# Fourier attention of a decoder layer: plain fp32 phases for the queries, and copies of key and query tiles placed ahead of the folds

## The reference, cut to what matters

```python
q = (x @ Wq.T + bq).reshape(B, L, 16, 32)        # 16 heads of 32; k and v likewise
def fourier(t):                                   # t: [B, L, 16, 32]
    p = einsum('blhd,dm->blhm', t, proj_mat) / sqrt(32)     # 128 phases for each head
    return concatenate([cos(p), sin(p)], -1) / sqrt(128)
kv  = einsum('blhm,blhd->bhmd', fourier(k), v)
out = einsum('blhm,bhmd->blhd', fourier(q), kv)
x   = layernorm(x + out.reshape(B, L, 512) @ Wo.T + bo)
```

## Time and profile before

| | |
|---|---|
| median of 3 runs | 1628.83 us (1627.93 to 1632.57) |
| profiled execution, its own time | 1629.87 us |
| its span in the trace | 1627.5 us |
| TensorE busy | 1564.6 us, 96% of the span |
| TensorE weight loads | 1116.4 us, 69% |
| VectorE busy | 1208.0 us, 74% |
| ScalarE busy | 1113.9 us, 68% |
| GpSimd busy | 715.5 us, 44% |
| mean granted TensorE clock | 0.991 |

### The profile page before, as it was taken

One profiled execution on the slowest core, in us unless ns is written; L12 is line 12 of the kernel. 1 busy time (PEld: TensorE's weight loads), 2 busy tenths in 40 slices (PEclk: granted clock), 3 DMA queues, 4 the chain that ended last, 5 costly groups with the idle time before them and its releaser, 6 DMA issues. The chain is left out here.

```text
span 1627.5 us, 29746 instructions
## 1 busy us (share of the span) xinstructions
PE 1564.6 (96%) x11188; PEld 1116.4 (69%) x11188; DVE 1208.0 (74%) x1849; ACT 1113.9 (68%) x1450; POOL 715.5 (44%) x633
## 2 busy tenths in 40 slices
PE   8999999999999999999999999999799999999996
PEld 6756765676676667667667766765478888888884
DVE  5687577668767766876776687898687777877876
ACT  5796677678667767867777786668256655565664
POOL 4233115203412410340232044373288978898886
PEclk9999999999999999999999999999899999999998
DMA  5100102201210220120022022001512222222211
GB/s 173 53 27 28 52 1 79 79 1 36 83 39 1 79 79 2 52 81 25 1 79 79 2 66 89 30 27 52 150 49 85 85 78 84 84 79 83 78 40 65
DMA packets 49175, 95.75 MB, mean 59 GB/s; under 512 B 3552, under 2 KB 3872, under 8 KB 49056
## 3 DMA queue, kind: packets, MB, share of 16 engines
q1 hardware_dynamic: 39776, 76.67, 15.0%
q10 hardware_dynamic: 9280, 17.31, 2.9%
HBM read 60.38 MB, written 33.59 MB: 58 GB/s over the span
## 5 line engine op out<-in xcount | busy, mean ns | idle before, releaser
L793 DVE SCALAR_TENSOR_TENSOR feat<-feat,phases 128x1024 f32<-128x1024 f32 x256 | 300.9, 1217 | 167.2 <-ACT feat L683 167.1
L683 ACT ACTIVATE feat<-phases 128x1024 f32<-128x1024 f32 x256 | 248.4, 1024 | 127.3 <-PE phases L533 108.2
L690 ACT ACTIVATE feat<-feat 128x1024 f32<-128x1024 f32 x256 | 271.7, 1062 | 74.8 <-DVE feat L793 66.0
L396 POOL TENSOR_TENSOR xt_hi<-xt_raw,singles 128x512 fp32r<-128x512 f32 x60 | 67.7, 1158 | 481.1 <-PE bank L525 451.0
L696 ACT ACTIVATE feat<-feat 128x1024 f32<-128x1024 f32 x256 | 257.2, 1046 | 8.8 <-DVE feat L800 8.4
L800 DVE TENSOR_SCALAR feat<-feat 128x1024 int32<-128x1024 int32 x256 | 209.6, 823 | 45.8 <-ACT feat L690 45.3
L418 POOL TENSOR_TENSOR res<-res,bo_all 128x512 f32<-128x512 f32 x60 | 75.5, 1283 | 211.0 <-DMA res<-x 210.7
L595 PE MATMUL kv_sum<-feat,v 128*32 128x256 f32 x2048 | 123.8, 382 | 0.0
L621 PE MATMUL kv_sum<-feat,kv_cols 128*32 128x512 f32 x1024 | 123.1, 598 | 0.0
L523 PE MATMUL bank<-xt_hi,win_hi 128*128 128x512 f32 x256 | 108.3, 423 | 7.9 <-DVE win_lo L745 7.9
L1305 ACT ACTIVATE xs<-xs,shift,rstd 128x512 f32<-128x512 f32 x96 | 71.5, 807 | 63.4 <-POOL shift L1168 63.4
(11 more groups left out here) (219 smaller groups left out, 3611.6 us busy)
## 6 DMA issues: line engine op xcount, KB each, us to landing
normed<-res SPq DMA_DIRECT2D x32, 513.0 KB, 4.2
xt_raw<-xT SPq DMA_DIRECT2D x15, 1024.0 KB, 7.3
res<-x SPq DMA_DIRECT2D x30, 512.0 KB, 4.2
xs<-normed SPq DMA_DIRECT2D x24, 513.0 KB, 3.9
out<-xs ACTq DMA_DIRECT2D x24, 512.0 KB, 2.8
feat<-normed SPq DMA_DIRECT2D x8, 513.0 KB, 3.8
out<-feat ACTq DMA_DIRECT2D x8, 512.0 KB, 2.8
xt_raw<-ctx SPq DMA_DIRECT2D x8, 256.0 KB, 3.6
```

Of the source, the lines that this page charges most:

```text
L683: act.activation(feat[2 * (w % 2) + p][:, 0, :], phases[:, 2 * p:2 * p + 2, :].rearrange("p h n -> p (h n)"), ACT.Identity, bias=ROUND).th ...
L690: act.activation(f[:, 1, :], f[:, 0, :], ACT.Sin, scale=-TWO_PI).then_inc(sin_done, 1)
L793: dve.scalar_tensor_tensor(f[:, 0, :], f[:, 0, :], ROUND, phases[:, 2 * p:2 * p + 2, :].rearrange("p h n -> p (h n)"), ALU.subtract, ALU.s ...
```

## The change

Queries are kept whole in fp32, as keys are, in two tiles `whole` that both share; VectorE alone writes them. `query_phases` multiplies the whole tile with the whole projection in plain fp32: four matmuls of 512 columns in place of twelve in fp32r. ScalarE's part of step Q goes, and so do the halves of the projection, with their two instructions and waits at the start. In the list, K and Q stand ahead of sin in the slots; TensorE has no work in "sin", so its own order stays as it is. Two slots at the start of the first batch and slots 14 and 15 of the tail keep their order.

```diff
     after = {
-        11: [sin(11), Q(1, 1), cos(11), norm(1, 0), norm(1, 1), V(0, 0), out(10)],
-        12: [sin(12), Q(1, 2), cos(12), V(0, 1), out(11)],
-        13: [sin(13), Q(1, 3), cos(13), W(0, 0), W(0, 1), out(12)],
-        14: [sin(14), K(0, 0), cos(14), W(0, 2), W(0, 3), stats(0), out(13)],
+        11: [Q(1, 1), sin(11), cos(11), norm(1, 0), norm(1, 1), V(0, 0), out(10)],
+        12: [Q(1, 2), sin(12), cos(12), V(0, 1), out(11)],
+        13: [Q(1, 3), sin(13), cos(13), W(0, 0), W(0, 1), out(12)],
+        14: [K(0, 0), sin(14), cos(14), W(0, 2), W(0, 3), stats(0), out(13)],
...
-        9: [sin(9), Q(0, 3), cos(9), W(1, 3), out(8), turned(1), stats(1)],
-        10: [sin(10), Q(1, 0), cos(10), out(9)],
+        9: [Q(0, 3), sin(9), cos(9), W(1, 3), out(8), turned(1), stats(1)],
+        10: [Q(1, 0), sin(10), cos(10), out(9)],
     }
...
-    hi_order = order_of("q", "out")
+    hi_order = order_of("out")
...
-        stack_at = nc.sbuf_base
-        stack_hi = [sb(f"stack_hi{r}", [P, CHUNK], F32R) for r in range(2)]
-        keys = [nc.alloc_sbuf_tensor_at(f"keys{r}", [P, CHUNK], F32, offset=stack_at + r * CHUNK * 4) for r in range(2)]
-        stack_lo = [sb(f"stack_lo{r}", [P, CHUNK], F32R) for r in range(2)]
+        whole = [sb(f"whole{r}", [P, CHUNK]) for r in range(2)]
...
-            def query_phases(hi, lo):
-                for n, (st, pr) in enumerate(((hi, proj_hi), (lo, proj_hi), (hi, proj_lo))):
-                    for h in range(HPG):
-                        rows = slice(DH * h, DH * h + DH)
-                        last = pe.matmul(phases[:, h, :], pr[rows, :], st[rows, :], start=(n == 0), stop=(n == 2))
+            def query_phases(of):
+                for h in range(HPG):
+                    rows = slice(DH * h, DH * h + DH)
+                    last = pe.matmul(phases[:, h, :], proj_whole[rows, :], of[rows, :], start=True, stop=True)
                 return last
...
-                    elif kind == "q":
-                        _, c, g = s
-                        b = bank[order.ring(mode, s, 2)]
-                        w = KPAIRS + c * GROUPS + g
-                        act.wait_ge(product_done, order.at(i, mode, s) + 1)
-                        wait(act, phase_ready, PAIRS_A * batch_of(i, s) + w - 1)
-                        act.activation(stack_hi[w % 2][:], b[:], ACT.Identity, bias=bias[kind][:, g:g + 1]).then_inc(hi_ready, 1)
...
-                    elif kind == "k":
+                    elif kind in ("k", "q"):
                         _, c, g = s
-                        w = c * GROUPS + g
+                        w = (0 if kind == "k" else KPAIRS) + c * GROUPS + g
                         dve.wait_ge(product_done, n + 1)
                         wait(dve, phase_ready, PAIRS_A * own + w - 1)
...
-                        dve.tensor_scalar(keys[w % 2][:], b[:], bias[kind][:, g:g + 1], None, ALU.add).then_inc(bank_free, 1)
-                    elif kind == "q":
-                        _, c, g = s
-                        w = KPAIRS + c * GROUPS + g
-                        dve.wait_ge(hi_ready, hi_order.at(i, mode, s) + 1)
-                        dve.scalar_tensor_tensor(stack_lo[w % 2][:], b[:], bias[kind][:, g:g + 1], stack_hi[w % 2][:].bitcast(F32),
-                                                 ALU.add, ALU.subtract).then_inc(bank_free, 1)
+                        dve.tensor_scalar(whole[w % 2][:], b[:], bias[kind][:, g:g + 1], None, ALU.add).then_inc(bank_free, 1)
```

More of the change, by code:

```diff
@@ L112, in attention_steps @@
     after = {
-        11: [sin(11), Q(1, 1), cos(11), norm(1, 0), norm(1, 1), V(0, 0), out(10)],
-        12: [sin(12), Q(1, 2), cos(12), V(0, 1), out(11)],
-        13: [sin(13), Q(1, 3), cos(13), W(0, 0), W(0, 1), out(12)],
-        14: [sin(14), K(0, 0), cos(14), W(0, 2), W(0, 3), stats(0), out(13)],
[L117 to L126, removed]
-        9: [sin(9), Q(0, 3), cos(9), W(1, 3), out(8), turned(1), stats(1)],
-        10: [sin(10), Q(1, 0), cos(10), out(9)],
+        11: [Q(1, 1), sin(11), cos(11), norm(1, 0), norm(1, 1), V(0, 0), out(10)],
+        12: [Q(1, 2), sin(12), cos(12), V(0, 1), out(11)],
+        13: [Q(1, 3), sin(13), cos(13), W(0, 0), W(0, 1), out(12)],
+        14: [K(0, 0), sin(14), cos(14), W(0, 2), W(0, 3), stats(0), out(13)],
+        15: [K(0, 1), sin(15), cos(15), V(0, 2), norm(0, 0), out(14), norm(0, 1)],
+        0: [K(0, 2), sin(0), cos(0), V(0, 3), out(15)],
+        1: [K(0, 3), sin(1), cos(1), V(1, 0), kv(0)],
+        2: [K(1, 0), sin(2), cos(2), V(1, 1), kv(1)],
+        3: [K(1, 1), sin(3), cos(3), V(1, 2), kv(2)],
+        4: [K(1, 2), sin(4), cos(4), V(1, 3), kv(3)],
+        5: [K(1, 3), sin(5), cos(5), W(1, 0), kv(4)],
+        6: [Q(0, 0), sin(6), cos(6), W(1, 1), kv(5)],
+        7: [Q(0, 1), sin(7), cos(7), save(0), W(1, 2), kv(6)],
+        8: [Q(0, 2), sin(8), cos(8), kv(7), turned(0), save(1)],
+        9: [Q(0, 3), sin(9), cos(9), W(1, 3), out(8), turned(1), stats(1)],
+        10: [Q(1, 0), sin(10), cos(10), out(9)],
     }
@@ L140, in attention_steps @@
         1: [K(0, 3), sin(1), cos(1), V(0, 2), V(0, 3), V(1, 0), kv(0)],
-        2: [sin(2), K(1, 0), cos(2), V(1, 1), kv(1)],
+        2: [K(1, 0), sin(2), cos(2), V(1, 1), kv(1)],
     }
@@ L148, in attention_steps @@
     after = {
-        12: [sin(12), Q(1, 2), cos(12), out(11)],
-        13: [sin(13), Q(1, 3), cos(13), W(0, 0), out(12)],
+        12: [Q(1, 2), sin(12), cos(12), out(11)],
+        13: [Q(1, 3), sin(13), cos(13), W(0, 0), out(12)],
         14: [sin(14), cos(14), W(0, 1), W(0, 2), wf(0), out(13)],
@@ L187, in attention @@
         wlo = {"k": kept.win_lo, "v": kept.wf_lo, "q": sb("wq_lo", [P, KD, D], F32R), "o": sb("wo_lo", [P, KD, D], F32R)}
-        proj_hi = sb("proj_hi", [P, MAP], F32R)
-        proj_lo = sb("proj_lo", [P, MAP], F32R)
         proj_whole = sb("proj_whole", [P, MAP])
@@ L245, in attention @@
         w_split = {m: sem(f"w{m}_split") for m in "vkqo"}
-        proj_hi_done, proj_split = sem("proj_hi_done"), sem("proj_split")
         wf_grid, wround, wq, win_stage, x_last = kept.xt_raw, scratch[:, 0, :], scratch[:, 1, :], v[0], v[1]
@@ L556, in batch @@
                         if s == ("phase", 0):
-                            pe.wait_ge(proj_split, 1)
+                            pe.wait_ge(scaled, 1)
                         if s == ("kvt", 0):
@@ L579, in batch @@
                         wait(pe, frac_ready, 2 * (PAIRS_A * own + w))
-                        last = key_phases(keys[w % 2]) if w < KPAIRS else query_phases(stack_hi[w % 2], stack_lo[w % 2])
+                        last = (key_phases if w < KPAIRS else query_phases)(whole[w % 2])
                         last.then_inc(phase_ready, 1)
@@ L919, in _ @@
             dve.tensor_scalar(proj_whole[:], proj_whole[:], TURNS, None, ALU.mult).then_inc(scaled, 1)
[L920 to L923, removed]
             dve.wait_ge(bias_in, BIASES)
```

## The result

The changed kernel takes 1612.87 us (median; 1612.14 to 1614.43), the kernel before beside it 1630.7: ratio 0.9888, 95% interval 0.9866 to 0.991. The forecast was 1621.8 us with a range of 1617 to 1629. The profiled execution of after has a time of 1614.43 us and a span of 1612.5, 15.0 less than before.

What follows compares the result with a forecast made beforehand. TensorE, busy 96% of the span, was taken as the bound, through its work and short waits. Dearer phases +11.1, removed waits -15.6, first batch -1.8, last -0.7 sum to -7.0 us: 1621.8 us, range 1617 to 1629.

Steps and rivals of the forecast that it cites:

- The waits: TensorE's waits for copies in slots 13, 14, 9 and ahead of Q go once copies precede folds: -15.6 us.
- The phases: Each plain fp32 query phase costs TensorE 0.21 us more, priced from the key phase; 53 on the path: +11.1 us.
- rival (b): Query phases get a third dearer, +0.30 us each, four terms for three: sum -2.2, 1626.6 us; chance 0.12.
- Rival (d): The row groups of the new query phases do not overlap on TensorE: 186 us slower; chance 0.02.
- First and last batch: Copy waits also go in the first and last batch: -1.8 us in the first, -0.7 us in the last.
- -0.7 us: Last batch: a wait goes, one-product slots gain, one beside GpSimd loses; range 0 to -2.
- one wait and a chain: Last batch: a 1.97 us wait goes, but a ScalarE and VectorE chain follows, with 1.56 us of waiting for fractions.
- Nothing of the second half changes: The kernel's second half, after the attention phases, keeps its time: 0 us.
- (a): Waits come back at the fractions ahead of the phases; with half of them back +0.8 us, 1629.6 us; chance 0.2.
- (c): Late cosines pass through ScalarE's queue to phases in slots 8 to 10: +8.5 us, 1637.3 us; chance 0.08.
- ScalarE loses its copy: 0: Taking 64 copies, 42.9 us, off ScalarE gains 0 by itself, since that engine is not the bound.

Runs made afterwards that it cites:

- split_first: Kernel before, queries still split in halves by ScalarE and VectorE, with the new order (copies ahead of folds) in every slot: 1602.94 us, ratio 0.9837.
- keys_first: Kernel before with only the key copies moved ahead of the folds; queries stay split and late: 1623.04 us, ratio 0.9965.
- padded: Changed kernel with the two removed VectorE instructions on the projection halves put back at the start, result unused: 1613.56 us, ratio 0.9899.
- after_pieces: Changed kernel with one second-half constant written by VectorE in 32 pieces, 31 instructions more and no buffer moved: 1613.02 us, ratio 0.9884.
- after_busy: Changed kernel with an idle copy put back on ScalarE between sine and cosine in slots 6 to 13: 1615.88 us, ratio 0.9909.

## Why the prediction was wrong, point by point

**The waits, "Gain: 10.9 + 2.4 + 1.6 + 0.7 = -15.6 us".** This term failed, in size. The mechanism was right: the copy follows the fractions at once, the bank is free in time, and every one of these waits went. But I took their price from the idle column, and that counts from the end of the last matmul. In a stream, matmuls start every 0.23 us and are shown 0.39 long, so 0.16 us of the wait lies under the last one; and the second matmul after a wait follows the first by 697.25 - 696.92 = 0.33 us instead of 0.23: together 0.26 us for each wait. Slot 13 of the batch shown waited 1.19 us by the column, and 12.63 - 11.14 = 1.49 by the starts of the phases. Over the six inner batches the new order gives 20.18 / 6 = 3.36 us a batch; I had 15.6 / 7 = 2.2. By slots, start to start against the idle column of those batches: 1.93 us against 1.62 in slot 13, 0.64 against 0.35 in slot 14, 0.33 against 0.26 in slot 9, 0.22 against 0.12 in slot 12, and 0.25 in slots 10 and 11, where TensorE's matmuls show no wait for a copy; what that last part is stays open. So this term alone misses 6 x 1.13 = 6.8 us of the 8.0 by which the span was off. The rest is -1.9 for cheaper phases in these batches, -0.6 in the first batch, -3.0 in the last, and +4.3 for the start and the second half.

The trace of before already showed why the column is too low. This is the row behind the wait of the earlier trace rows, timeline of TensorE:

```profile
697.25 0.39 PE L524 MATMUL bank<-wo_lo,att_hi 128*128 128x512 f32 x1
```

**The phases, +0.21 us x 53 = 11.1.** The nearest row, the key phase, was 0.04 too dear: 1.07 us against 1.11. The cost is 53 x 0.17 = 9.0 us, and the count of 53 holds: against split_first the changed kernel takes 8.12 us more in the inner batches (48 phases), 0.89 in the first (5), and nothing in the last. By rival (b) a phase would have cost 1.20 us; the trace has 19% more than the three terms, not 33%. Rival (d) fell with it: the row groups overlap. The four passes that the Trainium skill states (FP8 and Floating Point Precision, TensorE Precision Notes) would give the same 1.20, as an estimate; this trace does not agree.

**First and last batch.** The first gave 3.56 us where my terms make 3.0, and in the last "-0.7 us" failed: it gave 3.72. In both, the profiled execution of before had a spell of the lower clock, with matmuls of 0.63 us (from 100.9 us on, and from 1087.3 in slot 9 of the last batch), which the prediction had seen once and left inside the range. Windows of before (columns: stretch, length, busy time of TensorE, its weight loads, VectorE, ScalarE, GpSimd, clock, DMA share, GB/s):

```profile
92.00:108.00 16.00, 13.82 (x85) 7.89 (x86) 14.22 (x15) 14.14 (x16) 12.12 (x10) 0.89 0.07 17
1084.00:1100.00 16.00, 14.03 (x75) 9.22 (x76) 14.14 (x21) 12.39 (x14) 14.19 (x13) 0.89 0.19 63
```

After has 1.00 in the same stretch of the first batch, though TensorE still idles 1.58 us at 103.75 in it:

```profile
92.00:108.00 16.00, 13.96 (x88) 7.10 (x81) 13.20 (x17) 13.49 (x15) 12.20 (x10) 1.00 0.07 12
```

But the waits that the change removed do not decide it. keys_first still has them, and its clock stayed up (timeline of TensorE, then windows):

```profile
93.71 0.50 PE L523 MATMUL bank<-xt_hi,wq_hi 128*128 128x512 f32 x1 [1.42 <-DVE stack_lo L814]
...
101.64 0.50 PE L523 MATMUL bank<-xt_hi,wq_hi 128*128 128x512 f32 x1 [1.55 <-DVE stack_lo L814]
...
1079.86 0.50 PE L523 MATMUL bank<-xt_hi,wq_hi 128*128 128x512 f32 x1 [2.00 <-DVE stack_lo L814]
```

```profile
93.10:109.10 16.00, 13.84 (x92) 8.04 (x93) 14.22 (x14) 14.13 (x16) 12.13 (x10) 1.00 0.06 19
1078.00:1094.00 16.00, 14.14 (x88) 8.63 (x92) 15.11 (x23) 13.92 (x16) 15.32 (x15) 1.00 0.17 62
```

With the same waits, slot 10 of the first batch lasts 8.91 us before and 7.33 in keys_first, and slot 9 of the last 12.67 and 11.12. So the two spells cost 1.58 and 1.55 us, 3.1 of the 15.0. With equal waits on both sides, whether a spell falls there looks like chance; no second trace of before is kept. The Trainium skill (TensorE: Matmul & The Clock Gate, Part 1) says that the gate lowers the clock after idling; here waits of 1.42, 1.55 and about 2 us went with a drop in one trace and with none in the other. Over its executions before took 1626.6 to 1628.8 us where the mean clock was 0.994 or more, and 1631.7 to 1635.3 where it was 0.989 or less.

Without the spells the first batch gave 2.0 us and the last 2.2. In the last I had priced one wait and a chain, and missed that VectorE itself is the bound in slots 6 and 7, where it also prepares the weights. There the folds and the key copy stand in its way: 9.59 and 10.23 us a slot before, 8.68 and 9.27 after. VectorE's folds before and after:

```profile
L800 DVE TENSOR_SCALAR feat<-feat 128x1024 int32<-128x1024 int32 x256 | 209.6, 823 | 45.8 <-ACT feat L690 45.3
```

```profile
L786 DVE TENSOR_SCALAR feat<-feat 128x1024 int32<-128x1024 int32 x256 | 186.8, 771 | 1.5 <-ACT feat L683 1.5
```

The same 256 folds are 23 us less busy and no longer wait 45 us for the sine. Slots 10 and 11 give 1.6 us back: their next phases wait for fractions, as I had said of that chain (1.23 us at 1089.94).

**"Nothing of the second half changes"** missed 2.84 us, and the first phases came 1.5 us later. Both are in part the idle of VectorE ahead of its instructions: padded, without the first gap, starts its phases 1.2 us earlier, and of the second after_pieces took away 1.1 us. The rest stays open.

**The rivals.** (a) did not happen in the inner batches: their phases wait for nothing in after. (c) neither. The cosines do come later, as ScalarE's group shows (after):

```profile
L689 ACT ACTIVATE feat<-feat 128x1024 f32<-128x1024 f32 x256 | 258.5, 1052 | 39.7 <-DVE feat L786 39.7
```

Before, the cosines waited 8.8 us for the folds, now 39.7. But that stayed inside ScalarE's slack: slots 8, 10 and 12 have changed by +0.15, +0.07 and -0.05 us, with +0.17 for the phase in each. "ScalarE loses its copy: 0" was right for the inner batches in the new order, as after_busy shows, and wrong for the old one.

The miss of the span again, stretch by stretch from the table: -8.8 us in the inner batches, of which the price of the waits is 6.8 and the cheaper phases 1.9; -0.6 and -3.0 in the first and last batch, in which 3.1 us of lower clock went away, which looks like luck; +4.3 for start and second half. Together -8.0.

## What to carry to other kernels

Price a wait from start to start of the instruction that repeats, over a slot with it and one without, not from the idle column: here the waits of slots 13 and 14 were worth 0.3 us each more than the column said. Look up the granted clock of every stretch that is compared, since two spells at the lower clock made a fifth of this difference. When a change has two parts, run each alone before keeping both: here the order gave all the gain and the cheaper-looking copy cost a third of it. And when a buffer is added or resized, compare the interval between matmuls in the stages behind it, since their operands have moved.

## What was unexpected of the hardware

64 bytes per partition more, ahead of the buffers of the second half, made its 512-column matmuls start every 0.2331 us instead of 0.2279, at full clock in both (granted clock 1.00 from 1150 to 1570 us): 2.3%, and 7.3 us of that half. 160 bytes did the same (0.2333). Which buffers and which offsets matter was not tried. A comparison of two kernels whose buffers differ can carry such a term; here it did not part before from after, whose second halves both have 0.2279 us.
